# A step's reciprocal at its own end, and queries scaled on their way out of PSUM in the last group

## The reference

```python
x = x + cross_attention(layernorm(x), ctx, Wq, Wkv, Wout)   # 16 heads of 32, causal mask
x = x + moe(layernorm(x), ...)                              # 8 experts, the best 2 of a softmax, plus a gated shared expert
```

## Time and profile before

| | |
|---|---|
| median of 3 runs | 1511.88 us (1510.55 to 1513.28) |
| the profiled execution | 1511.73 us |
| its span | 1510.0 us |
| PE busy | 98% of the span |
| ACT busy | 43% of the span, 90% or more in nearly every slice of the first 380 us |
| DVE, POOL busy | 57%, 39% |
| granted clock, mean | 0.997 |

### The profile page before, as it was taken

How to read it: one execution, slowest core, us unless ns; L and a number is a source line. 1 busy time by engine, 2 the same in 40 slices (tenths; PEclk the granted TensorE clock), 3 DMA queues, 4 the chain that set the end, 5 groups by cost and what they waited for, 6 DMA issues and landing times.

```text
span 1510.0 us, 28303 instructions
## 1 busy us (share of the span) xinstructions
PE 1479.8 (98%) x10034; PEld 1257.8 (83%) x10034; DVE 857.0 (57%) x1460; ACT 653.8 (43%) x1836; POOL 588.6 (39%) x503
## 2 busy tenths in 40 slices
PE   6999999999999999999999999999999999999999
PEld 5888888888778899999999999787888888888887
DVE  5566777777765586786877867455223232223322
ACT  6999999999853323332332333332112121111211
POOL 3333455555562387595775864102101102011010
PEclk9999999999999999999999999999999999999999
DMA  7244434433365689877867864553203022031110
GB/s 241 71 118 117 116 108 121 117 101 112 86 139 111 182 307 336 277 245 263 286 229 273 283 211 175 183 194 97 85 15 112 28 73 60 7 112 28 64 48 28
DMA packets 102905, 217.44 MB, mean 144 GB/s; under 512 B 43696, under 2 KB 48816, under 8 KB 98064
## 3 DMA queue, kind: packets, MB, share of 16 engines
q1 hardware_dynamic: 91184, 184.71, 37.6%
q0 software_dynamic: 11616, 31.35, 7.2%
HBM read 168.86 MB, written 47.17 MB: 143 GB/s over the span
## 4 chain that ended last, share of the span: by engine, by line
PE 83%; ACT 9%; DVE 4%; issue 2%; DMA 1%; POOL 1%; DVEq 0%; POOLq 0%; ACTq 0%; SPq 0%
PE psum L823 60%; PE psum L1144 11%; ACT probs L1249 6%; PE psum L904 2%; PE psum L1046 2%; PE psum L954 2%; PE psum L945 1%; PE psum L1070 1%; PE psum L973 1%; ACT probsT L1238 1%; PE psum L1011 1%; DMA wj_raw<-in_w_shared 1%; PE psum L962 1%; PE psum L982 1%; DVE smax L1688 0%
## 5 line engine op out<-in xcount | busy, mean ns | idle before, releaser
L1561 POOL DMA_INDIRECT routed<-expert_out_dram,slot_b x56 | 56.4, 1006 | 480.2 <-DVE slot_b L2010 329.0
L1249 ACT ACTIVATE probs<-psum,minus_max,rs 112x112 f32<-112x112 f32 x512 | 222.1, 497 | 3.6 <-DVE minus_max L1690 3.4
L2028 DVE TENSOR_TENSOR h_s<-psum,silu_s 128x512 f32<-128x512 f32 x66 | 45.6, 692 | 302.5 <-PE psum L823 302.5
L823 PE MATMUL psum<-nT_hi,ws_hi 128*128 128x512 f32 x528 | 209.6, 397 | 3.2 <-DVE nT_lo L1951 2.9
L823 PE MATMUL psum<-nT_lo,ws_hi 128*128 128x512 f32 x528 | 209.2, 396 | 0.0
L823 PE MATMUL psum<-nT_hi,ws_lo 128*128 128x512 f32 x528 | 209.0, 396 | 0.0
L1533 POOL DMA_INDIRECT xg<-normed_dram,tile_ids x63 | 149.2, 2368 | 35.4 <-DMA tile_ids<-lists_dram 12.2
L823 PE MATMUL psum<-wj_hi,gT_hi 128*128 128x352 f32 x504 | 162.8, 323 | 0.0
L823 PE MATMUL psum<-wj_hi,gT_lo 128*128 128x352 f32 x504 | 162.3, 322 | 0.0
L823 PE MATMUL psum<-wj_lo,gT_hi 128*128 128x352 f32 x504 | 161.8, 321 | 0.0
L1369 ACT ACTIVATE silu_s<-psum 128x512 f32<-128x512 f32 x66 | 39.5, 598 | 244.8 <-PE psum L823 244.7
(11 more groups left out here) (253 smaller groups left out, 3433.7 us busy)
## 6 DMA issues: line engine op xcount, KB each, us to landing
wj_raw<-in_w_experts SPq DMA_DIRECT2D x35, 1408.0 KB, 6.6
wj_raw<-in_w_experts SPq DMA_DIRECT2D x35, 768.0 KB, 5.8
wj_raw<-in_w_shared SPq DMA_DIRECT2D x22, 768.0 KB, 5.8
expert_out_dram<-y_c SPq DMA_DIRECT2D x63, 256.0 KB, 3.1
base<-x_dram SPq DMA_DIRECT2D x8, 1024.0 KB, 5.8
xT_raw<-in_xT SPq DMA_DIRECT2D x32, 224.0 KB, 4.7
x_in<-in_x SPq DMA_DIRECT2D x32, 224.0 KB, 4.8
x_res<-in_x SPq DMA_DIRECT2D x32, 224.0 KB, 3.1
```

What stands on the lines that cost most here:

```text
L823: mm = pe.matmul(out_ap, u, v, start=(n == 0), stop=(n == last))
L1249: done = act.activation(probs[:, j % 2, 4 * r + m, :], psum[0:SEQ, r, m * SEQ:(m + 1) * SEQ], ACT.Exp, bias=minus_max[:, r, m:m + 1], scal ...
L1561: pool.indirect_dma_start(out=routed[:, b % 2, c, :], out_offset=None, in_=expert_out_dram, in_offset=bass.IndirectOffsetOnAxis(ap=slot_b[ ...
L2028: dve.tensor_tensor(h_s[:, :], bank(b), silu_s[:, :], ALU.mult).then_inc(emptied_b[b], 1)
```

## The change

- DVE takes the reciprocal of batch `t` at the end of step `t`, ahead of the `choices`, in place of the start of step `t+1`.
- In group 6, POOL spreads the factors of batches 28 to 31 over 128 columns (`root_wide`), PE transposes them into bank 6, and DVE copies them out (`rootT`). Both live in `xT_raw`. The four query tiles of group 7 leave PSUM on DVE, multiplied by `rootT`, and no longer on ACT. DVE does this at the start of the next step; the last one stands ahead of the reciprocal of step 27.
- In group 7 the exponentials take the constant `SCALE` as scale, and `minus_max` is the maximum times `-SCALE`.
- The factors of all batches have to be there by step 24. `mv1` and `rs1` get 12 slots. Steps 16 to 22 do two `stats1` and two `scaled_root` each, step 23 one, later steps none. SP loads `x_in` one step later than before in the first part, and two batches in a step from step 14 on.
- In group 7 POOL splits the second half of the contexts ahead of `rows` and the scatters, not behind.
- `gap_a` shrinks by the space of the new slots.

```diff
+    if _j == 0:
+        TURNS += [((_j, "root", 0), "last", 6)]
     TURNS += [((_j, "q", 0), -TB, 5), ((_j, "k", 0), -2, 7)]
...
+        root_wide = xT_raw[0:SEQ, 0:2, :, :].rearrange("s a k n -> s (a k n)")[:, 0:TB * P].rearrange("s (t p) -> s t p", t=TB)
+        rootT = xT_raw[:, 2, :, :].rearrange("p k n -> p (k n)")
...
+        def is_last_group(g):
+
+            return g == NG - 2
+
+        def statistics_in(t):
+
+            twice = NB - 4 * TB
+            n = [t + 1] if t < twice else [2 * t - twice + 1, 2 * t - twice + 2]
+            return [i for i in n if i < NB]
...
-                    if there(g, j, -TB):
-                        load_x(t + TB)
+                    for n in statistics_in(t + 2):
+                        load_x(n)
...
+                if is_last_group(g) and j == 0:
+                    pe.wait_ge(S["roots_spread"], 1)
+                    b = take(g, j, "root")
+                    for i in range(TB):
+                        mm = pe.transpose(psum[:, b, i * SEQ:(i + 1) * SEQ], root_wide[:, i, :], ident[0:SEQ, 0:SEQ])
+                    mm.then_inc(filled[b], 1)
...
-                                                          bias=minus_max[:, r, m:m + 1], scale=rs1[:, j % 2, 1:2],
+                                                          bias=minus_max[:, r, m:m + 1], scale=SCALE if g == NG - 1 else rs1[:, t % (3 * TB), 1:2],
...
-                    if there(g, j, -TB):
+                    if there(g, j, -TB) and not is_last_group(g):
                         evacuate(g, j, "q", 0, qT[(g + 1) % 2], (j,), 0, GT)
...
-                inverse_root(mv1, rs1, t % 2, "stats1", "rstd1_made", t + 1, SCALE ** -2)
+                inverse_root(mv1, rs1, t % (3 * TB), "stats1", "rstd1_made", t + 1, 1.0 if t >= NB - TB else SCALE ** -2)
...
+                    if j == 0 and g == NG - 1:
+                        split_context(2 * g + 2, g, 1)
+                    if is_last_group(g) and j == 0:
+                        pool.wait_ge(S["xT_split"], NB - 2)
+                        pool.wait_ge(S["rstd1_made"], 2 * NB)
+                        settled(pool)
+                        pool.tensor_copy(root_wide, rs1[:, TB:2 * TB, 1].unsqueeze(2).to_broadcast([SEQ, TB, P])).then_inc(S["roots_spread"], 1)
...
-                    if j == 0 and before(g, NG):
+                    if j == 0 and before(g, NG - 1):
                         split_context(2 * g + 2, g, 1)
...
-                    if there(g, j, -1):
-                        scaled_root(t + 1)
+                    for n in statistics_in(t):
+                        scaled_root(n)
...
+            def roots_out():
+                b = turns.bank("root")
+                wait_filled(dve, NG - 2, 0, "root")
+                dve.tensor_copy(rootT, bank(b, P, GT)).then_inc(emptied[b], 1)
+
+            def queries_out(j):
+
+                b = turns.bank("q")
+                wait_filled(dve, NG - 2, j, "q")
+                wait_emptied(dve, NG - 2, 0, "root")
+                dve.tensor_tensor(qT[(NG - 1) % 2][:, j, :], bank(b, P, GT), rootT, ALU.mult).then_inc(emptied[b], 1)
...
-                if there(g, j, 1):
-
-                    dve.wait_ge(S["exp_done"], 2 * t)
-                    if there(g, j, 2):
-                        dve.wait_ge(S["rinv_spread"], t - 1)
-                    dve.reciprocal(rinv[:, :], rsum[:, (j + 1) % 2, :]).then_inc(S["rinv_made"], 1)
+                if is_last_group(g) and j:
+                    if j == 1:
+                        roots_out()
+                    queries_out(j - 1)
...
+                        if g == NG - 1:
+                            dve.tensor_scalar(minus_max[:, 2 * i:2 * i + 2, :], smax[:, 2 * i:2 * i + 2, :], -SCALE, None, ALU.mult).then_inc(S["max_made"], 1)
...
-                if there(g, j, -1):
-                    stats1(t + 1)
+                for n in statistics_in(t):
+                    stats1(n)
...
+                if is_last_group(g) and j == TB - 1:
+                    queries_out(j)
+                if there(g, j, 0):
+
+                    dve.wait_ge(S["exp_done"], 2 * t + 2)
+                    at_least(dve, S["rinv_spread"], t)
+                    dve.reciprocal(rinv[:, :], rsum[:, j % 2, :]).then_inc(S["rinv_made"], 1)
                 if is_late(g, 0) or not is_late(g, 2) or (j < TB - 1 and not is_late(g)):
                     choices(g, j)
```

More of the change, by code:

```diff
@@ L75, in there @@
             return 2 <= g < self.batches // TB
+        if lag == "last":
+            return g == self.batches // TB - 2
         if lag == "tail":
@@ L171, in build_program @@
         stat1, stat2 = sa("stat1", [SEQ, 6]), sa("stat2", [SEQ, 6])
-        mv1, mv2 = sa("mv1", [SEQ, 2, 2]), sa("mv2", [SEQ, 2, 2])
-        rs1, rs2 = sa("rs1", [SEQ, 2, 2]), sa("rs2", [SEQ, 2, 2])
+        mv1, mv2 = sa("mv1", [SEQ, 3 * TB, 2]), sa("mv2", [SEQ, 2, 2])
+        rs1, rs2 = sa("rs1", [SEQ, 3 * TB, 2]), sa("rs2", [SEQ, 2, 2])
         smax = sa("smax", [SEQ, 4, 4])
@@ L210, in build_program @@
         wout_hi, wout_lo = sa("wout_hi", [P, KC, C], F32R), sa("wout_lo", [P, KC, C], F32R)
-        sa("gap_a", [P, 464])
+        sa("gap_a", [P, 416])
         n0_hi, n0_lo = sa("n0_hi", [P, KC, ST], F32R), sa("n0_lo", [P, KC, ST], F32R)
@@ L291, in build_program @@
             "ctx_loaded ctx_hi_made ctx_split "
-            "mean_step wq_centred xT_split stats1 rstd1_made stats2 rstd2_made xn2_ready "
+            "roots_spread mean_step wq_centred xT_split stats1 rstd1_made stats2 rstd2_made xn2_ready "
             "smax_made max_made scores_done exp_done xT_hi_made attnT_hi_made attnT_split rinv_made rinv_spread "
@@ L580, in _ @@
             sp.dma_start(gates_sb[:, :, :].rearrange("p k e -> p (k e)"), gates).then_inc(S["gates_loaded"], 16)
-            for t in range(1, TB):
+            for t in range(1, 3):
                 load_x(t)
@@ L1578, in stats1 @@
             def stats1(t):
-                at_least(dve, S["rstd1_made"], 2 * (t - 1))
+                at_least(dve, S["rstd1_made"], 2 * (t - 3 * TB + 1))
                 dve.wait_ge(x_loaded[t % TB], 16 * (t // TB + 1))
-                stats(x_in[:, t % TB, :], stat1, mv1, t % 2, "stat1_raw", "stats1", t + 1)
+                stats(x_in[:, t % TB, :], stat1, mv1, t % (3 * TB), "stat1_raw", "stats1", t + 1)
             def centre(half):
@@ L1689, in step @@
                         dve.wait_ge(S["smax_made"], 2 * t + i + 1)
-                        dve.tensor_scalar(minus_max[:, 2 * i:2 * i + 2, :], smax[:, 2 * i:2 * i + 2, :], rs1[:, j % 2, 1:2], -1.0, ALU.mult, ALU.mult).then_inc(S["max_made"], 1)
+                        if g == NG - 1:
+                            dve.tensor_scalar(minus_max[:, 2 * i:2 * i + 2, :], smax[:, 2 * i:2 * i + 2, :], -SCALE, None, ALU.mult).then_inc(S["max_made"], 1)
+                        else:
+                            dve.tensor_scalar(minus_max[:, 2 * i:2 * i + 2, :], smax[:, 2 * i:2 * i + 2, :], rs1[:, t % (3 * TB), 1:2], -1.0,
+                                              ALU.mult, ALU.mult).then_inc(S["max_made"], 1)
                 if is_late(g) and (g == NG - 1 or (g == NG and j == 0)):
```

## The result

The changed kernel takes 1513.74 us (median of 22 runs, 1511.15 to 1520.02), the kernel before 1511.51 (22 runs, 1508.44 to 1514.86). The ratio is 1.0018, 95% interval 1.0011 to 1.0025: 1.7 to 3.8 us slower, where I had forecast 0.8 us faster. The profiled execution takes 1513.59 us, 1.86 more than that of before, with a span of 1511.7 us and a clock of 0.997.

What follows compares the result with a forecast made beforehand. PE was taken to bound phase A, except steps 29 to 31, where ACT's exponentials do. Terms -0.4 + 0.1 + 2.4 - 2.9 = -0.8 us gave 1511.1 us, range 1505.0 to 1515.2 (the forecast's own 1508.5 to 1513.5).

Steps and rivals of the forecast that it cites:

- What bounds the kernel: PE sets phase A's pace except steps 29 to 31 (ACT); an ACT and DVE loop limits gains in groups 2 to 5.
- The reciprocal, -0.4 us: Groups 2 to 5: PE's 3.5 us of `rinv_wide` waits go, mostly reappearing before the ranks; ends 0 and -3.5.
- The statistics, +0.1 us: Steps 16 to 22: a second `stats1` on DVE slightly delays the ranks; ends 0 and +0.9.
- Group 6, +2.4 us: Queries leave bank 5 behind the choices, delaying the transposes and exponentials of steps 25 and 26; ends 0.5 and 3.5.
- The four extra transposes of PE are inside this wait: Group 6: PE's added transposes, some 0.6 us, fall inside step 25's 1.6 us wait for bank 5.
- Group 7, -2.9 us: Steps 28 to 31: cheaper exponentials; `xn` wait replaces `ctx_lo` wait, clock falls again; 42.2 us against 45.1; ends 0, -5.1.
- My 75: Group 7: the constant scale saves 75 ns per exponential, 1.2 us a step.
- A: Faster: groups 2 to 5 keep 3.5 us, queries leave in time, clock doesn't fall; -6.8, 1505.1 us; chance 0.28.
- C: Group 7: the constant scale is worth nothing, so its 2.9 us are gone; 1514.0 us; chance 0.13.
- B: Slower: POOL's spread beside DVE's choices stalls ten steps in groups 2 to 6, 0.41 us each; +4.1, 1515.2 us; chance 0.12.
- The sum: Whole kernel: -0.4 + 0.1 + 2.4 - 2.9 = -0.8 us, median to 1511.1 us; chance 0.47.

Runs made afterwards that it cites:

- experiment 7: Changed kernel with the ranks in bank 5, between projection and router, and DVE taking them out ahead of the residual; ratio 1.0012 (1.0000 to 1.0024).
- 2: Changed kernel with the reciprocal back at the start of the next step; ratio 0.9993 (0.9985 to 1.0002), median 1510.34 us.
- experiment 10: Kernel before with the reciprocal at its own step's end, and POOL splitting contexts behind `scaled_root` in groups 0 to 6; ratio 0.9998 (0.9988 to 1.0007).
- 5: Changed kernel with 64 more idle waits early in PE's program; ratio 1.0006 (0.9995 to 1.0016), median 1512.85 us.
- 9: Changed kernel with roots and queries out of PSUM ahead of `aT_lo`, and POOL's group 6 scatters behind the first maxima; ratio 0.9997 (0.9988 to 1.0006).
- experiment 1: Kernel before with only the reciprocal moved to the end of its own step; ratio 1.0010 (1.0000 to 1.0020), median 1512.79 us.
- 4: Kernel before with the statistics part alone (slots, double statistics, SP's loads); ratio 0.9995 (0.9985 to 1.0005).
- second trace of before: Kernel before run once more, unchanged, for a second trace; ratio 0.9999 (0.9988 to 1.0010).
- 8: Changed kernel with the reciprocal at its old place and roots and queries out of PSUM ahead of `aT_lo`; ratio 0.9970 (0.9959 to 0.9980), median 1507.45 us.
- experiment 3: Changed kernel with roots and queries taken out of PSUM in the step that makes them, ahead of `aT_lo`; ratio 1.0012 (0.9999 to 1.0024).

## Why the prediction was wrong, point by point

**What bounds the kernel.** Right as far as the runs go. The waits for `rinv_wide` went, their 3.5 us did not come back, and another bank for the ranks, behind `rinvT`, did not let PE keep them (experiment 7). That ACT's and DVE's loop sets groups 2 to 5 is read from the timeline and agrees with every run; no run took the loop away.

**The reciprocal, -0.4 us: the step that failed.** With it, groups 2 to 5 lost 2.2 us and more was lost behind them; with the old place and all else the same they lost 0.06 (2). Both ends of my range for it, 0 and -3.5, excluded a loss. I wrote that the order of reciprocal and choices "doesn't change" the loop's length, and looked only for what PE would wait for next. I did not ask which work of POOL moves with the reciprocal. Three things are found. (a) POOL's split of the contexts came to lie beside the choices: +0.5 us in step 10 (experiment 10). In groups 3 to 5 the lag grows by 0.1 to 0.2 us over the same step, with the split out of the way too. (b) A piece of PE's program came to be fetched behind SP's burst: 1.2 us in step 16 (shown by 5; why the early reciprocal loses this race is not shown). (c) POOL's scatters moved from beside the values' products, where nobody waits for PE's signal, to beside the scores and the first transposes of steps 25 and 26, where ACT and DVE wait for it (9). In the changed kernel (c) overlaps the wait for the queries' bank: steps 24 to 26 lose 3.7 us there and 3.1 with the late reciprocal (2). Alone, in experiments 1 and 10, step 26 shows it with 1.3 us. Of the 2.2 us in groups 2 to 5, (a) and (b) make 1.7; the other 0.5 us are spread over steps 14 to 24 and no run takes them apart.

**The statistics, +0.1 us.** Right: 0.07 (4), 0.06 (2). In the changed kernel the router waits 0.4 us for `xn2T` in steps 18 and 22; without the early reciprocal (2, 4) it waits 0.13 us at most.

**Group 6, +2.4 us.** It lost 3.5 by the two windows. By the starts of the exponentials of steps 24 and 28 it is 3.3, and 3.1 against the second trace of before, which has late signals as well. The queries behind the choices were seen rightly: 0.9 and 1.2 us of waits in steps 25 and 26. "The four extra transposes of PE are inside this wait" was wrong. They come a step earlier, in series: 0.81 us for bank 6, which DVE frees with `logits`, and 0.34 us of PE. With the late reciprocal group 6 still lost 2.7 us (2); with the queries early 0.6 (8).

**Group 7, -2.9 us.** It gained 5.1. The waits are as forecast: 1.32 us for `xn` at step 28, none for `ctx_lo`. Three sizes were off. The clock did not fall behind this wait, in this trace or in any of the seven others with the split moved; step 28 is 1.4 us shorter for it (I had the fall at 1.15 us). For step 29 I took PE's busy time of before, 10.63 us, as the least it can take; the same 136 matmuls are now busy for 10.02, so that busy time was no lower bound. And the constant scale is worth more than 75 ns. The exponentials, by line in the last 40 us of phase A:

```profile
L1271 ACT ACTIVATE probs<-psum,minus_max 112x112 f32<-112x112 f32 x64 | 22.1, 436 | 0.0
L1271 ACT ACTIVATION_READ_ACCUMULATOR probs<-psum,minus_max 112x1 f32 x64 | 18.5, 290 | 0.0
```

```profile
388.03 0.41 ACT L1271 ACTIVATE probs<-psum,minus_max 112x112 f32<-112x112 f32 x1
388.27 0.26 ACT L1271 ACTIVATION_READ_ACCUMULATOR probs<-psum,minus_max 112x1 f32 x1
388.36 0.41 ACT L1271 ACTIVATE probs<-psum,minus_max 112x112 f32<-112x112 f32 x1
```

One takes 436 ns and before 511 (mean of the same 64): 75 ns, as I said. But they overlap, and the pace is what counts: one starts every 329 ns (0.33 here), before every 422. That is 93 ns, 1.5 us a step, and step 31 takes 8.35 us where I had 8.6. The Trainium skill, page ScalarE: Activation LUTs, section What ACT_TABLE_LOAD costs, names about 93 ns for a pointer operand. The distance of the starts agrees with that (93 ns), the difference of the durations does not (75 ns), and by the page step 31 came out as 8.3 us. My 75 was worked out from durations, and I took it for the pace. Steps 29 and 30 are PE's, 10.02 and 9.73 us busy of 10.16 and 10.07.

**The rivals.** A (faster) did not come: from step 8 to 24 no trace with the early reciprocal is shorter than that of before, also with the ranks behind `rinvT` (7) or the split out of the way (10). C fell with the constant scale. B (slower) had the right sign and the right neighbours, POOL beside DVE's choices, and the wrong sum: the lag grows by 0.5 us in one step, behind the context split, and by some 0.2 or less in the others, not by 0.41 in ten. POOL's spread of the reciprocal itself, which B blamed, does hold DVE: by 0.11 us in step 9 (L1839, in 10 as well), 0.12 in steps 13, 17 and 25, 0.35 in 20 and 21, and 0.42 in the last step of groups 2 to 5. The lag shows little of it (0.1 us or less over steps 11, 15 and 19). The Trainium skill, page SBUF — State Buffer, its terms, has the loser of the shared port blocked for a whole instruction. These rows agree: each of the held operations ends 0.02 to 0.05 us behind the end of POOL's instruction, so what it loses is what was left of that instruction when it came. Which operations are held is narrower than I took it. The reduction at 148.66 (0.19 us) inside the spread is not, and beside POOL's `xn` (2.08 us) `aT_lo` takes 1.03 us in place of 0.6, as if it were held until 0.65 us after `xn` began and not to its end.

**The sum.** By the trace: +0.5 from the start to step 8 (the clock, on the whole), +2.2 for steps 8 to 24, +3.5 for group 6, -5.1 for group 7 and +0.7 behind it make 1.8 us. My terms were 0, -0.3, +2.4 and -2.9. These are differences of single traces: the two of the kernel before end 1.4 us apart (spans of 1510.0 and 1508.6), so that the +0.5 and the +0.7, for which I have no cause in the change, are not firm. The median lay inside the range, just under C (1514.0) and just above the forecast's own 1508.5 to 1513.5; its side was wrong. That it came within 2.6 us of the forecast is partly luck: the reciprocal and group 6 cost 3.6 us more than I had, and group 7 brought 2.2 more.

## What to carry to other kernels

When an instruction of an engine with slack is moved forward, list what its consumers do next and beside whom: here the gain was stopped by a loop that the move did not touch, and POOL's next instructions then fell on DVE's chain and on PE's signals. Put an added evacuation where its engine already waits (DVE ahead of `aT_lo`), not behind its longest chain: with the reciprocal back in its place, that took the kernel from 0.9993 to 0.9970, while with the early reciprocal the late signals ate it (1.0018 to 1.0012). And price an operand by the distance of starts, not by durations, where instructions overlap.

## What the runs showed of the hardware

- PE's signals can come late while POOL issues indirect DMAs: up to 2.1 us behind PE's row in step 25, about 0.5 us behind the end of the second scatter, and gone from this step when the scatters were moved (9). That POOL's issue is what holds them is shown by this one move; the mechanism inside is not. In experiment 3 the scores' signal came inside the second scatter, so the end of the scatter is not a strict bound. One trace of fourteen, the first of the kernel before, has scatters without late signals.
- PE can run dry of program. A 16 KB piece that came behind some 6 us of stores and loads left PE standing for 1.2 us, and with 64 idle instructions ahead of it the piece came before the burst and PE did not stand (5). The Trainium skill, page Runtime: NRT & Kernel Launch, section Instruction fetch mechanics, has pieces of 16 KiB, as queue 8 shows, but 128 KiB of instruction memory for PE and a cost that is mostly hidden. The trace does not fit that: a piece that came some 170 PE instructions late was enough to stop PE, and that is less than one piece.
- VectorE is held by some GpSimd instructions to their end: an addition of 0.17 us took 0.52 beside `ctx_lo` and ended 0.03 us behind it (changed kernel; the same in experiment 1).
- A wait of 1.0 us was followed by a fall of PE's clock to 1.2 GHz for 3.4 us in both traces of the kernel before (387.5 and 387.0 us), and in none of four other kernels with the same wait. Two traces of one kernel agreeing did not make it a property of the wait.
